# Gated cross-attention with experts: query matmuls one step earlier, their evictions ahead of the exponential, one null row, and new deals of statistics and maxima

## What is computed

```python
def _L0_xattn_ref(x, context, mask, ...):
    xn = _ln(x, ln1_s, ln1_b)
    cn = _ln(context, lnc_s, lnc_b)
    q = xn @ Wq
    k, v = jnp.split(cn @ Wkv, 2, axis=-1)
    k = jnp.concatenate((nk, to_heads(k)), axis=2)      # one null key ahead of the 1500
    v = jnp.concatenate((nv, to_heads(v)), axis=2)
    sim = jnp.einsum('bhid,bhjd->bhij', to_heads(q) * h ** -0.5, k)
    attn = jax.nn.softmax(jnp.where(mfull, sim, max_neg), axis=-1)
    out = jnp.einsum('bhij,bhjd->bhid', attn, v).transpose(0, 2, 1, 3).reshape(b, n, h * d) @ Wo
    return _ln(out, lno_s, lno_b)

x = x + jnp.tanh(g_xattn[0]) * xattn(_layernorm(x), ctx, mask, ...)
x = x + jnp.tanh(g_ffn[0]) * ffn(_layernorm(x), ...)   # the expert of the largest score, gelu between w1 and w2
```

## Time and profile before

| | us |
|---|---|
| median of 3 runs | 750.47 |
| lowest and highest of them | 749.02, 750.52 |
| the profiled execution, its own time | 749.7 |
| its span, first to last instruction | 747.9 |
| PE busy | 696.9 (93%) |
| DVE busy | 570.1 (76%) |
| ACT busy | 509.6 (68%) |
| POOL busy | 388.7 (52%) |

### The profile page before, as it was taken

How to read it: one execution, slowest core, us unless ns; L and a number is a source line. 1 busy time by engine, 2 the same in 40 slices (tenths; PEclk the granted TensorE clock), 3 DMA queues, 4 the chain that set the end, 5 groups by cost and what they waited for, 6 DMA issues and landing times.

```text
span 747.9 us, 14835 instructions
## 1 busy us (share of the span) xinstructions
PE 696.9 (93%) x5041; PEld 396.2 (53%) x5041; DVE 570.1 (76%) x1001; ACT 509.6 (68%) x650; POOL 388.7 (52%) x462
## 2 busy tenths in 40 slices
PE   3698989999989998999899989998999899899997
PEld 2454444455544544454445444544454445468886
DVE  4976878787877786878787878787878675877776
ACT  1416676767676766676767676767676767687895
POOL 6654567773727372737373737273737235656200
PEclk9759999999999999999999999999999999999999
DMA  5825091726080606060616061616121201010000
GB/s 158 176 68 56 1 124 43 123 44 85 26 84 25 84 25 84 25 81 28 74 34 82 27 75 34 81 27 79 29 43 25 42 26 57 26 27 2 12 4 14
DMA packets 73992, 40.33 MB, mean 54 GB/s; under 512 B 61309, under 2 KB 68501, under 8 KB 73957
## 3 DMA queue, kind: packets, MB, share of 16 engines
q1 hardware_dynamic: 73525, 39.77, 32.8%
q10 hardware_dynamic: 432, 0.10, 0.1%
HBM read 26.65 MB, written 0.52 MB: 36 GB/s over the span
## 4 chain that ended last, share of the span: by engine, by line
PE 68%; ACT 12%; DVE 11%; issue 5%; DMA 2%; POOL 1%; ACTq 0%; SPq 0%; DVEq 0%; POOLq 0%
PE S L1208 23%; PE A L1228 21%; PE X L1266 9%; ACT S L675 5%; ACT PP L680 4%; PE S L1365 4%; PE A L1382 3%; DVE mx L1006 3%; DVE PP L961 2%; DMA raw<-ctx_dram 2%; PE X L1382 1%; DVE st L999 1%; ACT nullrow L703 1%; PE X L1276 1%; PE A L1151 1%
## 5 line engine op out<-in xcount | busy, mean ns | idle before, releaser
L675 ACT ACTIVATE S<-S,mb 125x896 f32<-125x896 f32 x192 | 187.7, 977 | 168.8 <-PE S L1208 168.8
L961 DVE TENSOR_TENSOR PP<-S,PP 125x896 f16<-125x896 f32 x192 | 209.3, 1091 | 98.5 <-ACT PP L680 92.6
L1006 DVE TENSOR_REDUCE mx<-X 128x1 f32<-128x500 f32 x336 | 212.1, 669 | 11.7 <-PE X L1266 9.7
L1228 PE MATMUL A<-PP,z_hi 125*128 125x448 f16 x768 | 206.4, 353 | 3.5 <-ACT Af L759 3.5
L680 ACT ACTIVATE PP<-S 125x896 f16<-125x896 f32 x192 | 175.2, 912 | 4.9
L1266 PE MATMUL X<-zTh,qh 128*128 128x500 f16 x336 | 134.5, 406 | 17.9 <-DVE ql L982 11.6
L1228 PE MATMUL A<-PP,z_lo 125*128 125x448 f16 x384 | 121.7, 353 | 0.0
L1228 PEld LDWEIGHTS A<-PP,z_hi 125*128 125x128 f16 x768 | 74.5, 98 | 75.5 <-ACT Af L759 5.8
L1208 PE MATMUL S<-qh,zTh 128*128 128x448 f16 x384 | 104.6, 354 | 1.7 <-DVE PP L961 1.7
L1208 PE MATMUL S<-qh,zTl 128*128 128x448 f16 x384 | 104.0, 352 | 0.0
L1208 PE MATMUL S<-ql,zTh 128*128 128x448 f16 x384 | 104.0, 353 | 0.0
(11 more groups left out here) (202 smaller groups left out, 1185.5 us busy)
## 6 DMA issues: line engine op xcount, KB each, us to landing
raw<-ctx_dram SPq DMA_DIRECT2D x16, 750.0 KB
Rb<-r_scratch SPq DMA_DIRECT2D x16, 448.0 KB, 3.5
wst<-in_w_dram SPq DMA_DIRECT2D x16, 256.0 KB, 3.0
early<-in_Wkv_dram SPq DMA_DIRECT2D x2, 512.0 KB, 14.2
early<-in_Wq_dram SPq DMA_DIRECT2D x1, 512.0 KB, 5.6
Wo_s<-in_Wo_dram SPq DMA_DIRECT2D x1, 512.0 KB, 11.7
zTh<-z_hi SPq DMA_TRANSPOSE x32, 3.7
zTl<-z_lo SPq DMA_TRANSPOSE x32, 3.8
```

Source lines behind the costliest of these rows:

```text
L675: act.activation(s, s, ACT.Exp, bias=mb[:, p, c:c + 1]).then_inc(e_done, 1)
L961: dve.tensor_tensor(Pl[:, k, :].rearrange("p (a r) -> p a r", a=2), S[0:CK, 2 * (c % 2):2 * (c % 2) + 2, 0:HR], Ph[:, k, :].rearrange("p ( ...
L1006: dve.reduce_max(mx4[:, np_].rearrange("q k t -> q (k t)")[:, j:j + 1], X[:, j % 2, 0:KB], AX).then_inc(mx_red, 1)
L1228: ins = mm(A[:, a, 0:HR], z[:, p, c, :], q[:, k, a * HR:(a + 1) * HR], start=(c == 0 and n < 2), stop=(c == NC - 1 and n >= 4))
```

## The change

- PE: both halves of the queries of batch b+2 move from step 10 (behind `sim` of the next batch's chunk 0) to the end of step 9 (behind `pv` of chunk 9), except in batch -1.
- ACT: in step 10 the two `query_hi` come first, ahead of the exponential of the next batch's chunk 0. The two null rows of 448 become one instruction over both banks (`queries_null`, 1x896), behind the high part of that chunk; it waits for both `ql`.
- DVE: both `ql` come in step 10 ahead of `sub`, and wait for `qhi_done` instead of `null_done`.
- PE waits for `null_done` where `X` is overwritten: ahead of the first maximum, and ahead of `project`.
- The statistics of batch b+3 are all made in batch b: four each in steps 8, 9 and 11, ahead of `sub`. Steps 0 and 1 have none left.
- The 21 maxima are dealt 3-3-2-3-2-3-2-3 to steps 0 to 7 instead of 2-3-3-3-3-3-3-1.

```diff
-        MAXIMA = {0: (0, 1), 1: (2, 3, 4), 2: (5, 6, 7), 3: (8, 9, 10), 4: (11, 12, 13), 5: (14, 15, 16),
-                  6: (17, 18, 19), 7: (20,)}
+        MAXIMA = {0: (0, 1, 2), 1: (3, 4, 5), 2: (6, 7), 3: (8, 9, 10), 4: (11, 12), 5: (13, 14, 15), 6: (16, 17),
+                  7: (18, 19, 20)}
+        STATS = {8: range(0, 4), 9: range(4, 8), 11: range(8, 12)}
...
+            def queries_hi(n, p):
+
+                for j in range(2):
+                    query_hi(n, p, j, X[:, j, 0:HR])
+
+            def queries_null(n):
+
+                act.wait_ge(null_in, 16 * n)
+                act.wait_ge(qlo_done, 2 * n + 2)
+                act.activation(nullrow[0:1, :].rearrange("o (a r) -> o a r", a=2), X[0:1, :, 0:HR], ACT.Identity,
+                               scale=1.0 / W_SCALE, bias=rowbias[0:1, 0:1]).then_inc(null_done, 2)
...
-                    queries_early = c >= 10 and f["znext"] and f["main"] and (f["y"] or c == 11)
+                    if c == 10 and f["znext"] and f["main"]:
+                        queries_hi(b + 2, p)
...
-                    if queries_early:
-                        queries(b + 2, p, c - 10)
                     if exp_slot:
                         exps_hi(*ahead(b, c))
+                    if c == 10 and f["znext"] and f["main"]:
+                        queries_null(b + 2)
...
-                    late = c == 10 and not f["y"]
-                    if c >= 10 and f["znext"] and not late:
-                        queries(b + 2, p, c - 10)
-                    if c == 9 and f["load"]:
-                        context_stats(b + 3, 1 - p, range(HC), 16 * ((b - p) // 2 + 2 + p) if isinstance(b, int)
+                    if c == 10 and f["znext"] and f["main"]:
+                        queries(b + 2, p, 0)
+                        queries(b + 2, p, 1)
...
+                    if c in STATS and f["load"]:
+                        context_stats(b + 3, 1 - p, STATS[c], 16 * ((b - p) // 2 + 2 + p) if isinstance(b, int)
...
-                    if c < 2 and f["main"]:
-                        if f["znext"]:
-                            context_stats(b + 2, p, range(HC + 3 * c, HC + 3 * c + 3), None)
...
                             pe.wait_ge(qlo_done, 2 * nb + 2)
+                            pe.wait_ge(null_done, 2 * nb + 2)
...
-                if c == 10 and part >= 1 and f["znext"]:
-                    queries(b + 2, p, part - 1, True)
+                if c == (9 if f["main"] else 10) and part == 2 and f["znext"]:
+                    queries(b + 2, p, 0, True)
+                    queries(b + 2, p, 1, True)
...
                             pe.wait_ge(qlo_done, 2 * b + 5)
+                            pe.wait_ge(null_done, 2 * b + 6)
```

More of the change, by code:

```diff
@@ L732, in body @@
                         act.activation(b1T[:, :], A[:, 1, 0:E * FC], ACT.Copy).then_inc(b1_copied, 1)
-                    if c == 10 and f["znext"] and not queries_early:
+                    if c == 10 and not f["main"]:
                         queries(b + 2, p, 0)
@@ L977, in take_y, with queries @@
                                          ALU.add).then_inc(y_done, 2)
-            def queries(n, p, j, banks=X):
-                dve.wait_ge(null_done, 2 * n + j + 1)
+            def queries(n, p, j, banks=X, early=False):
+                if early:
+                    dve.wait_ge(null_done, 2 * n + j + 1)
+                else:
+                    dve.wait_ge(qhi_done, 2 * n + j + 1)
                 dve.scalar_tensor_tensor(ql[:, p, j * HR:(j + 1) * HR], banks[:, j, 0:HR], rowmask[:, 0:1],
@@ L1021, in body @@
                                           negate=True).then_inc(mneg_done, 1)
-                    late = c == 10 and not f["y"]
-                    if c >= 10 and f["znext"] and not late:
-                        queries(b + 2, p, c - 10)
-                    if c == 9 and f["load"]:
-                        context_stats(b + 3, 1 - p, range(HC), 16 * ((b - p) // 2 + 2 + p) if isinstance(b, int)
+                    if c == 10 and f["znext"] and f["main"]:
+                        queries(b + 2, p, 0)
+                        queries(b + 2, p, 1)
+                    if c == 11 and not f["main"]:
+                        queries(b + 2, p, 1, early=True)
+                    if c in STATS and f["load"]:
+                        context_stats(b + 3, 1 - p, STATS[c], 16 * ((b - p) // 2 + 2 + p) if isinstance(b, int)
                                       else (b - p) * 8 + 32 + 16 * p)
@@ L1029, in body @@
                         sub(*ahead(b, c))
-                    if f["znext"] and late:
-                        queries(b + 2, p, c - 10)
+                    if c == 10 and not f["main"]:
+                        queries(b + 2, p, 0, early=True)
                     if f["prep"]:
@@ L1054, in body @@
                         take_y(b, 0)
-            queries(0, 0, 0, S[:, 2:4, :])
-            queries(0, 0, 1, S[:, 2:4, :])
+            queries(0, 0, 0, S[:, 2:4, :], early=True)
+            queries(0, 0, 1, S[:, 2:4, :], early=True)
             for b in (-1, 0, 1):
```

## The result

The changed kernel takes 765.5 us (median of 4 runs, 764.7 to 765.9), the kernel before 750.5. The ratio on record is 1.018 (interval 1.0159 to 1.020), that of these two medians 1.020. It is slower, as forecast, but by 15 us, where the sum had said 8.8. The kernel before was run again beside each group of experiments and gave medians of 752.2, 752.3 and 752.9; against those the change costs 13 us. The span of the profiled execution grew from 747.9 to 762.9.

What follows compares the result with a forecast made beforehand. PE, read by starts, stands still 3.5 us a batch without projection, 1.5 with, the turn's holes behind ACT. 8 x (1.01 - 0.75 + 0.05) + 6 x (1.60 - 0.6 + 0.05) = 8.8; forecast 758.7, range 754 to 763 (wide 749.5 to 767).

Steps and rivals of the forecast that it cites:

- rival 4: Queries issued slowly behind their wait, or the old number of late maxima: 8 to 10 us on top, 768; chance 0.14.
- The break-even: At the turn: the summed effect changes sign at D = 1.52, a shift-row wait of 0.3 us instead of 0.9.
- D: Delay of the next batch's first `sim`, forecast 2.15; a turn costs D - 1.84 without projection, D - 1.10 with it.
- The turn: From step 9 to the next batch's first `pv`: `pv` starts 0.82 later without projection, 1.40 later with it.
- Steps 1 to 7: Fewer late maxima and no statistics there: 20.4 and 20.5 us, gains of 0.75 without and 0.6 with projection.
- Step 8: The join of the maxima stands one reduction (0.6) later behind `sub`, PE one and a half maxima later: 0.05 lost.
- The ends: First and last batches: batch 0 gains a little more, batch 14 less; set against each other.
- Rival 1: The turn gets shorter, so faster; without any wait for the shift row -4 us, 745.7; chance 0.13.
- Rival 2: The maxima cease to wait at all: 10 us of the loss come back, 749, no change; chance 0.08.
- Rival 3: Nothing on PE changes its length: same 5041 matmuls, its queue hides the new waits, 749.7; chance 0.07.

Runs made afterwards that it cites:

- shift_first: Changed kernel with ACT's shift row copied ahead of the exponential of chunk 11 in step 9: 749.1 us, ratio 0.9955.
- null_early: Changed kernel with the null row ahead of the high part of the next batch's chunk 0: 760.3 us, ratio 1.010.
- turn_only: Changed kernel with maxima and statistics dealt as before; queries, evictions, null row and their waits as changed: 768.3 us, ratio 1.022.
- stats_only: Kernel before with only the statistics moved, four each in steps 8, 9 and 11: 748.4 us, ratio 0.9949.
- deal_only: Kernel before with only the new deals of maxima and statistics: 751.7 us, ratio 0.9997.
- best_old_maxima: shift_null_early with the maxima dealt as before (2-3-3-3-3-3-3-1), statistics as changed: 742.1 us, ratio 0.9858.
- join_sooner: shift_null_early with the maxima dealt 3-3-2-3-3-3-2-2, so step 7 has two: 743.6 us, ratio 0.9883.
- shift_null_early: Changed kernel with both the shift row ahead of chunk 11's exponential and the null row ahead of chunk 0's high part: 744.9 us, ratio 0.9902.

## Why the prediction was right, and where its size was off

**The mechanism held, term by term.** The forecast was a wait of 0.9 ahead of the queries in every turn, ended by the shift row; a projection that waits some 0.8 for the null row; a first `pv` that still waits for `Af`; a turn that loses more than the steps win. The trace shows each, and shift_first, null_early and turn_only each price one of them. By range it was a near thing: 765.5 lies 2.5 above the narrow range (754 to 763, given 0.58) and 1.5 inside the wide one (749.5 to 767), and rival 4's 768 is nearer to it than the 758.7 forecast (which by its own sum, 758.5 and 0.8 for the median, should have been 759.3).

**The break-even was only half confirmed.** It was put at a delay D of the first `sim` of 1.52, and D = 1.24, no wait at all, at 4 us faster than before. shift_first has D = 4.66 - 3.42 = 1.24 and is 0.45% faster, some 3 us. That agreement is luck. The forecast at this D was 0.60 less and 0.14 more a batch; measured are 0.23 less and 0.47 more, so the batches are 1.0 us longer in all, and the total has the other sign; 1.7 us at a lower clock in the profiled execution of the kernel before are shown, the rest is likely of the same kind. The prediction had no such term. D moves the batches as it said: 2.33 to 1.24 took off 1.09.

**The sum was too small, on both sides of it:** 8.8 against 15.0 by the spans and 16.2 by the batches. The turn: forecast 0.82 and 1.40 a batch, 15.0 us in all; turn_only shows 1.08 and 1.83, 19.6 us. Four terms were too short. The wait was 1.0 and not 0.9. The 48 matmuls behind it took 1.33 (363.15 to 364.48) and not 1.24; the prediction had left between 1.24 and 2.26 open and chosen the lower end, and 0.09 is what the restart costs. The null row takes 0.98, where it had been priced by the shift row, the same 1x896 at 0.89. The type is not what sets them apart: `Af` is written as fp32 and takes 0.89 as well. Shift row and `Af` are plain copies; the null row adds a bias from SBUF, as the exponential does, and that takes 0.98. So the better row stood beside the one chosen. And the projection behind its wait takes 2.73 and not 2.68. In the turn without projection these make 0.28 of the first `pv`'s time (12.70 against a forecast of 12.42), in the one with projection 0.32 (14.16 against 13.84).

**The steps: forecast 0.5 and 0.35 a batch given back, 0.22 and 0.27 found.** This is the term *Steps 1 to 7* with *Step 8*. Without projection steps 1 to 7 took 20.59 and not 20.4, a gain of 0.58 and not 0.75, and the join cost 0.15 and not 0.05. With projection they took 20.58 (336.29 to 356.87) and not 20.5. From the changed kernel's trace alone the 7.4 us missing by the batches are 4.2 of the turn, 1.9 of steps 1 to 7 and 1.3 of the join. The step that failed is the reading of the old lateness: 1.2 of late maxima against 0.7 was put down to the deal of maxima and statistics together, and in it the alternation to three and two was counted as a relief. The single changes tell otherwise: the statistics carry what was won (idle in steps 1 to 7 from 1.22 to 0.84, in stats_only as in deal_only), the maxima's deal wins nothing beside them and costs 0.15 by the join (best_old_maxima, join_sooner). The join was mis-sized because the wait of the join for the reduction ahead of it on the same engine (0.20 in the rows above) was left out: in the kernel before a `sub` stood between them.

**The ends** were set against each other, and that nearly held: the first two turns cost 0.31 and 0.15 less than those in the middle, the stretches ahead and behind 1.0 more. What the prediction had nowhere is the 1.7 us that the profiled execution of the kernel before, its starting point, lost at a lower clock.

**The rivals.** Rival 1 (a turn that gets shorter) was no property of this change, but one line away from it: in shift_first the wait it hung on is gone and the total is faster, but at full clock the turn is not shorter by what it named (above); the batches of both kinds get shorter than before only with the null row moved as well (shift_null_early, by 0.35 and 0.15). Rival 2 (no late maxima) fell: 65 of 111 late weight loads remain, and the time is 16 us away from it. Rival 3 (nothing on PE gets longer) fell with the 14 waits that PE's queue did not hide. Rival 4's first half, queries issued slowly behind a wait, is true with a tenth of its price: 0.09 instead of up to 1.0. Its sign, more than 1.3 us from the first to the last, is just reached: 1.30 from start to start (363.15 to 364.45). Its second half, as many late maxima as before, is half true.

**The busy share.** PE's share fell from 93% to 92%, while its idle time by starts went from 3.5 to about 4.4 us in a batch without projection (37.85 less the same 33.5 of work) and from 1.5 to 3.1 in one with it. Read by the share, almost nothing happened.

## What to carry to other kernels

Before moving work to an earlier place in one engine's queue, look at what it waits for and count the work that stood between the two: here `pv` and `sim`, 2.3 us, had hidden a wait for a row copied behind an exponential. Then look whether the producer has a gap ahead of the place where it makes that row; moving the small producer up was worth 1.1 us a batch. And try the parts of a bundled change one by one: here the statistics won 0.4 us in a batch without projection, the maxima's deal cost 0.15 in the new turn, and the turn wins (0.11 and 0.48 a batch, best_old_maxima against stats_only) only once both its waits are gone. Last, read such parts from batches at the same granted clock: the totals here put a kernel ahead whose batches were behind.

## What the runs showed of the hardware that was not expected

A short burst behind a wait restarts cheaply: 48 matmuls of 56 columns took 1.33 us instead of 1.24, although their wait stands in the sequencer (an ISA row) and not in the first matmul, and 48 of 128 columns took 2.73 instead of 2.68. On ACT 896 elements a row from PSUM took 0.89 to 0.92 us as a plain copy, written as fp16 (shift row, high part) or as fp32 (`Af`), and more where the instruction also reads a bias: 0.98 the null row, 0.94 to 0.99 the exponential; of 448 elements a row it is 0.54 (as fp16 and as fp32) and, in the null row of the kernel before, 0.61. No run changed the bias alone. And a reduction that reads what the reduction right ahead of it on DVE has written started 0.20 us after that one's end (0.19 to 0.20 in the three joins looked at). And a turn with waits of 1.36 and 0.45 us was at times followed by 3 to 4 us at a granted clock near the lower level, 1.3 to 1.7 us lost, in six batches of the four profiled executions with that turn. The turns of the changed kernel, with waits of 1.0, 1.01 and 0.84, and those of best_old_maxima, with one of 1.77, had none.
